# A graph, mixer and expert kernel on Trainium2: tokens go to expert-owned pages inside the graph network, sums are cleared by ScalarE, a bias add stands later

## The chip, the cores and the metric

The kernel runs on one core of a Trainium2 chip. The metric is the device time of one execution in microseconds (us), the median of several runs. The engines are TensorE (PE, with PEld for its weight loads), VectorE (DVE), ScalarE (ACT), GpSimd (POOL) and SyncE (SP), which issues most of the transfers. Every time of a stretch below is counted from the start of the profiled span.

## The reference, cut to what matters

Three parts work on 6250 tokens of 256 features: a graph network on the normalised tokens with per-node edge sums, a mixer of four layers, and at the end an expert layer that sends each token to one of 32 experts.

```
xn = layernorm(x)
x = x + gnn(xn, segment means of 106250 edge rows) + mixer(xn)     # 4 layers of linear attention and a feed-forward part
z = layernorm(x)
idx = argmax(z @ router_w.T + router_b)                            # one of 32 experts for each token
h = relu(z @ W1[idx] + b1[idx])                                    # 256 -> 64
x = x + relu(h @ W2[idx] + b2[idx])                                # 64 -> 256
```

## The kernel before, in words

Tokens lie as 50 tiles of P = 125 rows; two tiles make a group, so there are 25 groups (`GROUPS`). Each engine has its own program, and semaphores order them; nothing is scheduled by a planner. `res[P, 50, 260]` holds the residual rows with four more columns (layernorm scale and shift, token number, expert).

The mixer runs layer by layer. In its last layer each step also handles six of 153 edge segments, whose sums collect in `agg`. GpSimd clears `agg` at the start of that layer (line 795), and VectorE adds the graph network's output bias to the mixer's last bias there (`graph_bias`, line 1383), before the first group.

**The graph stage** follows. On each engine it is a loop over turns `i`, in which every step works on a group some turns behind: on GpSimd `res += x` for group `i` (line 847) and the reciprocal root for the layernorm of group `i-4` (line 850); on VectorE, the residual and statistics of group `i-4`, the shift that needs GpSimd's root (line 1787), the logits, the best expert and the one-hot `chosen` of group `i-6`; the running count `before_j` gives each token its rank within its partition's own column of experts. TensorE's products of the two graph layers fill the turn. SyncE loads `x` for group `g` when group `g-2` is used (`load_x`), and the experts' weights between (`load_experts`).

**The sort** comes after the last group: VectorE and TensorE work out the exclusive counts, the 1600-wide masks `fmask` and `fprod` and the positions `fpos_i`; then GpSimd scatters the 50 tiles in a row (line 854) into `tokens_sorted` in DRAM, in the order of the experts, without gaps. SyncE waits for all 50 (`f_scat`) before it loads anything.

**The expert loop** takes 81 segments (`FSEGS`): a tile of 125 sorted rows with one expert each. SyncE reads the first row's number and loads the tile `yin`; ScalarE normalises it to `zs` and copies the expert's weights; TensorE transposes and multiplies; VectorE adds; GpSimd scatters the rows to the output (line 864). Rows of the tile that belong to another expert get a number out of bounds (`omiss`). A tile with a border between experts is loaded once for each.

The lines that carry the order of these waits:

```
    for i in range(GROUPS + 4):                          # GpSimd, graph stage, before
        if i < GROUPS:
            pool.wait_ge(N_IN[i % 2], 16 * (i // 2 + 1))
            nc.gpsimd.tensor_tensor(pair(res, i), pair(res, i), x_in[i % 2], ALU.add).then_inc(n_x, 1)
        if i >= 4:
            pool.wait_ge(n_ve, i - 3)
            nc.gpsimd.tensor_tensor(..., gve, tail_half, ALU.pow).then_inc(n_root, 1)
    pool.wait_ge(f_posi, 1)
    for t in range(TILES): nc.gpsimd.indirect_dma_start(out=tokens_sorted, ...)
```

## Time and profile before

| | |
|---|---|
| median of 3 runs | 2889.43 us (2884.46 to 2896.06) |
| the profiled execution | 2899.41 us, its span 2897.7 us |
| TensorE busy | 2634.7 us, 91% |
| VectorE busy | 2147.9 us, 74% |
| ScalarE busy | 1578.4 us, 54% |
| GpSimd busy | 1762.0 us, 61% |
| TensorE's mean granted clock | 0.954 |

The profile is of one execution. A busy share is an average over stages that have different limits, so each stage is read by itself: a table of stretches says which engine fills one, the timeline says what an engine waited for, and the chain that ended last says which of these waits set the end.

### The profile page before, as it was taken

How to read it: one execution, taken by the hardware profiler on the slowest of the kernel's cores; microseconds unless marked ns; L12 is line 12 of the kernel's file. 1: busy time of each engine (PE TensorE's matmuls, PEld its weight loads, DVE VectorE, ACT ScalarE, POOL GpSimd, SP SyncE). 2: the span in 40 equal slices, each digit the busy share in tenths (PEclk: the TensorE clock that was granted, in tenths of full speed). 3: DMA queues.
4: the chain of work that ended last, by engine and by line, in shares of the span. 5: the costliest groups of instructions: out<-in, count | busy, mean ns of one | idle time of the engine just before them, and what ended most of it. 6: DMA issues, size and time to landing. Idle time of an engine off the chain costs nothing.

```text
span 2897.7 us, 57777 instructions
## 1 busy us (share of the span) xinstructions
PE 2634.7 (91%) x19546; PEld 2465.9 (85%) x19546; DVE 2147.9 (74%) x4892; ACT 1578.4 (54%) x3079; POOL 1762.0 (61%) x1615
## 2 busy tenths in 40 slices
PE   5888999999989999998999999799999998994398
PEld 3667899999989999998999999689999898994365
DVE  8988677777767777776777777688888886894154
ACT  0545466666636666663666666344444445762164
POOL 2045587777788777778877777555545553223565
PEclk7999999999999999999999999899999998996698
DMA  6012322222242222224223222343333332201343
GB/s 127 29 49 53 97 63 66 64 58 61 52 114 60 63 66 62 62 47 116 62 61 70 61 59 47 85 118 89 86 90 89 89 78 59 61 29 35 86 128 82
DMA packets 255569, 207.99 MB, mean 72 GB/s; under 512 B 165505, under 2 KB 194386, under 8 KB 255277
## 3 DMA queue, kind: packets, MB, share of 16 engines
q1 hardware_dynamic: 197678, 162.55, 21.6%
q0 software_dynamic: 57600, 41.75, 7.3%
q8 instruction: 160, 2.62, 0.4%
q14 instruction: 131, 1.07, 0.1%
HBM read 136.93 MB, written 70.16 MB: 71 GB/s over the span
## 4 chain that ended last, share of the span: by engine, by line
PE 62%; DVE 14%; POOL 11%; issue 9%; ACT 2%; DVEq 1%; DMA 1%; SPq 0%; another core or an unknown queue 0%; POOLq 0%; ACTq 0%
PE bank L399 57%; POOL edges_sorted L787 7%; PE bank L1915 4%; DVE hidh_lo L1391 3%; POOL tokens_sorted L854 2%; DVE xh L1355 2%; DVE scr L1265 1%; DVE oh L1588 1%; PE bank L2378 1%; POOL ehl L804 1%; DVEq L1567 1%; DVE bn L1346 1%; POOL r L765 1%; DMA queries<-qn 1%; DVE bn_x L1191 1%
## 5 line engine op out<-in xcount | busy, mean ns | idle before, releaser
L787 POOL DMA_INDIRECT edges_sorted<-staging,pos_i x850 | 1073.1, 1263 | 246.5 <-issue 230.1
L911 ACT ACTIVATE hid<-bank,b1p 128x250 f32<-128x250 f32 x800 | 331.1, 465 | 323.7 <-PE bank L399 281.1
L399 PE MATMUL bank<-w_hi,hidh_hi 128*125 128x256 f32 x1600 | 472.2, 295 | 24.1 <-DVE hidh_lo L1391 23.7
L399 PE MATMUL bank<-h_hi,w_hi 128*128 128x250 f32 x1600 | 479.7, 300 | 2.1 <-DVE h_lo L1375 1.3
L1391 DVE TENSOR_TENSOR hidh_lo<-hid,hidh_hi 128x500 fp32r<-128x500 f32 x400 | 319.5, 799 | 182.6 <-ACT hidh_hi L917 150.3
L399 PE MATMUL bank<-w_hi,hidh_lo 128*125 128x256 f32 x1600 | 454.1, 284 | 0.0
L399 PE MATMUL bank<-w_lo,hidh_hi 128*125 128x256 f32 x1600 | 452.3, 283 | 0.0
L399 PE MATMUL bank<-h_hi,w_lo 128*128 128x250 f32 x1600 | 448.9, 281 | 0.0
L399 PE MATMUL bank<-h_lo,w_hi 128*128 128x250 f32 x1600 | 445.4, 278 | 0.0
L399 PEld LDWEIGHTS bank<-w_hi,hidh_hi 128*125 128x125 f32 x1600 | 301.0, 188 | 32.9 <-DVE hidh_lo L1391 29.9
L399 PEld LDWEIGHTS bank<-h_hi,w_hi 128*128 128x128 f32 x1600 | 304.6, 190 | 6.5 <-DVE h_lo L1375 2.9
L917 ACT CAST hidh_hi<-hid 128x500 fp32r<-128x500 f32 x400 | 243.8, 610 | 117.2 <-PE bank L399 81.3
L399 PEld LDWEIGHTS bank<-h_lo,w_hi 128*128 128x128 f32 x1600 | 305.7, 191 | 1.9
L399 PEld LDWEIGHTS bank<-w_lo,hidh_hi 128*125 128x125 f32 x1600 | 300.6, 188 | 2.1
L399 PEld LDWEIGHTS bank<-h_hi,w_lo 128*128 128x128 f32 x1600 | 302.2, 189 | 0.0
L399 PEld LDWEIGHTS bank<-w_hi,hidh_lo 128*125 128x125 f32 x1600 | 299.9, 187 | 0.0
L765 POOL TENSOR_TENSOR r<-ve,minus_half 125x2 f32<-125x2 f32 x175 | 134.5, 769 | 228.8 <-DVE ve L1351 226.3
L804 POOL TENSOR_TENSOR ehl<-staging,ehl 128x512 fp32r<-128x512 f32 x103 | 139.3, 1352 | 155.4 <-ACT ehl L1003 147.6
L1588 DVE TENSOR_TENSOR oh<-iota_node,kb 128x1000 fp32r<-128x1000 f32 x153 | 192.1, 1255 | 41.0 <-POOL kb L799 40.7
L924 ACT COPY qT<-bank 128x500 f32<-128x500 f32 x100 | 57.7, 577 | 278.5 <-PE bank L1915 275.8
L399 PE MATMUL bank<-xh,ek 125*128 125x256 f32 x800 | 194.4, 389 | 6.8 <-DVE acc L1488 4.1
L399 PE MATMUL bank<-mmat,qT 128*125 128x256 f32 x800 | 190.0, 380 | 3.6 <-issue 3.6
(292 smaller groups left out, 6635.9 us busy)
## 6 DMA issues: line engine op xcount, KB each, us to landing
staging<-edges_sorted SPq DMA_DIRECT2D x103, 260.0 KB
staging<-in_edge_attr SPq DMA_DIRECT2D x50, 531.2 KB
queries<-qn SPq DMA_DIRECT2D x100, 250.0 KB
qin<-queries SPq DMA_DIRECT2D x100, 250.0 KB
edges_sorted<-staging,pos_i POOLq DMA_INDIRECT x850
rows_in<-edges_sorted SPq DMA_DIRECT2D x50, 260.0 KB
yin<-tokens_sorted SPq DMA_DIRECT2D x81, 127.0 KB
raw<-in_L_mix_W SPq DMA_DIRECT2D x8, 1024.0 KB, 5.8
```

Of the source, the lines that this page charges most:

```text
L399: return nc.tensor.matmul(o, left, right, start=start, stop=stop, skip_group_check=True)
L765: nc.gpsimd.tensor_tensor(o[:, :], ve[:, :], minus_half[:, :], ALU.pow).then_inc(done, 1)
L787: nc.gpsimd.indirect_dma_start(out=edges_sorted, out_offset=bass.IndirectOffsetOnAxis(ap=pos_i[:, i:i + 1], axis=0), in_=stage[:, slot, j, ...
L804: nc.gpsimd.tensor_tensor(ehl[n % 4][:, :, EA + 2:2 * EA + 2], rows_in[n % RIN][:, :, 0:EA], f32(ehl[n % 4][:, :, 0:EA]), ALU.subtract).th ...
L854: nc.gpsimd.indirect_dma_start(out=tokens_sorted, out_offset=bass.IndirectOffsetOnAxis(ap=fpos_i[:, t:t + 1], axis=0), in_=res[:, t, :], i ...
L911: a = nc.scalar.activation(hid[c % 2][:, j, :], chunks(PH[c % 2])[:, j, :], ACT.Gelu, bias=b1p[:, 2 * c + j:2 * c + j + 1])
L917: nc.scalar.copy(hidh[c % 2][0][:, :, :], hid[c % 2][:, :, :]).then_inc(f_hi, 1)
L924: nc.scalar.copy(qT[:, :, :], chunks(PQT)).then_inc(q_copied, 1)
L1355: a = nc.vector.tensor_scalar(o[:, j, :], res_row(PAIR * g + j), mv[:, j, 0:1], r[:, j:j + 1], ALU.subtract, ALU.mult)
L1391: nc.vector.tensor_tensor(hidh[c % 2][1][:, :, :], hid[c % 2][:, :, :], f32(hidh[c % 2][0][:, :, :]), ALU.subtract).then_inc(f_lo, 1)
L1588: nc.vector.tensor_tensor(oh[n % 4][:, :, :], iota_node[:, :].unsqueeze(1).to_broadcast((128, SEGR, P)), kb[:, n % 4, :].unsqueeze(2).to_b ...
L1915: a = nc.tensor.transpose(o[0:128, c, j * n:(j + 1) * n], i[:, j, c * 128:(c + 1) * 128], ident[0:n, 0:n])
```

## The change

It has four parts.

1. `tokens_sorted` is now 32 regions of 50 pages of 128 rows (`BIN` = 6400 rows, `YROW` = 264 columns), one region for each expert. A token's place needs only its expert and its rank within that expert, so it is known as soon as its group is routed. TensorE works out the ranks with six small BF16 products in each turn (`rank_tokens`), summed in the bank PQT; VectorE turns them into a rank and a page (`route_rank` to `route_page`), and GpSimd into an element number (`token_slots`) and scatters the tile inside the graph stage (`scatter_tile`). A scatter writes the rows of two tiles side by side, 2112 bytes for each token: its own row and, on the slot before it, a row that is overwritten later or masked. Since the slots overlap, each scatter waits until the one before it has landed. SyncE first fills page 0's slot of all regions with some row (`blank`): 128 x 32 rows.
2. After the loop only the page table is worked out, from 32 counts. The expert loop has 80 segments of 128 rows, read with a stride of 50 rows; the mask `fmiss` is worked out ahead.
3. ScalarE clears `agg`, at the end of the drain before the last layer, with a copy of zeros.
4. `graph_bias` stands behind the first group's `attention_low`.

TensorE's 48 idle products before the expert loop become 24, and no longer wait for the scatters' end.

```diff
+            blank = tokens_sorted.rearrange("(e p k) c -> p e k c", e=EXP, p=PAGE)[:, :, PAGES - 1, :]
+            sp.wait_ge(f_ones, 3)
+            sp.dma_start(blank[0:P, :, :], res[:, TILES - 1, :].unsqueeze(1).to_broadcast((P, EXP, YROW))).then_inc(blank_written, 16)
+            sp.dma_start(blank[P:PAGE, :, :], res[0:PAGE - P, TILES - 1, :].unsqueeze(1).to_broadcast((PAGE - P, EXP, YROW))).then_inc(blank_written, 16)
...
-                    nc.gpsimd.memset(agg[:, :, :], 0.0).then_inc(s_ones, 1)
...
+            def scatter_rows(at_rows, rows, done):
+                pool.wait_ge(f_scat, 16 * done)
+                nc.gpsimd.indirect_dma_start(out=token_cells, out_offset=bass.IndirectOffsetOnAxis(ap=at_rows, axis=0),
+                                             in_=rows, in_offset=None).then_inc(f_scat, 16)
+
+            def scatter_tile(t):
+                if t == 0:
+                    pool.wait_ge(blank_written, 64)
+                    scatter_rows(fpos_i[:, 0:1], res[:, 1, :], 0)
+                    scatter_rows(first_own[:, :], res[:, 0, :], 0)
+                else:
+                    scatter_rows(fpos_i[:, t:t + 1], res[:, t - 1:t + 1, :].rearrange("p t c -> p (t c)"), t + 1)
+
+            for i in range(GROUPS + 8):
+                if i >= 8:
+                    scatter_tile(PAIR * (i - 8) + 1)
...
-                if i >= 4:
+                if 4 <= i < GROUPS + 4:
                     pool.wait_ge(n_ve, i - 3)
                     nc.gpsimd.tensor_tensor(pair(res, i - 4, D + 1)[:, :, D], gve[:, :], tail_half[:, :], ALU.pow).then_inc(n_root, 1)
-            pool.wait_ge(f_posi, 1)
-            for t in range(TILES):
-                nc.gpsimd.indirect_dma_start(
...
+                if 7 <= i < GROUPS + 7:
+                    token_slots(i - 7)
+                    scatter_tile(PAIR * (i - 7))
...
+                if L == LAYERS - 1:
+                    act.wait_ge(c_ready, LAYERS)
+                    cells = agg[:, :, :].rearrange("p t c -> p (t c)")
+                    nc.scalar.copy(cells, tri[0:P, 0:1].to_broadcast((P, TILES * (2 * EA + 2)))).then_inc(s_ones, 1)
...
-                if l == LAYERS - 1 and t == -1:
-                    graph_bias()
...
                     attention_low(l, t + 1)
+                    if l == LAYERS - 1 and t == -1:
+                        graph_bias()
...
+            def route_page(g):
+                stepped()
+                if g >= 2:
+                    dve.wait_ge(f_scat, 16 * (PAIR * (g - 2) + 2))
+                nc.vector.tensor_scalar(page[:, g % 2, :], share[:, :], RND, None, ALU.add).then_inc(n_placed, 1)
...
+            def rank_tokens(g):
+                now, last = chosen[g % 2], chosen[(g + 1) % 2]
+                both = "p j e -> p (j e)"
+                pe.wait_ge(n_chosen, g + 1)
+                pe.wait_ge(n_placed, g)
```

How the instructions stand on three engines, before and after:

SyncE, at the start of the graph stage. Before:

```order
L693 DMA staging<-in_L_ffn_router_w 32x256 [waits s_add,f_res]
L694 DMA staging<-in_L_ffn_b 32x64
L695 DMA rb_b<-in_L_ffn_router_b 125x32
L632 DMA x_in<-in_x 125x512 [waits n_xn,n_x]
L699 DMA fw<-in_L_ffn_b 1x8192
L702 DMA fw<-in_L_ffn_W 128x4x64 x2
```

After:

```order
L707 DMA staging<-in_L_ffn_router_w 32x256 [waits s_add,f_res]
L708 DMA staging<-in_L_ffn_b 32x64
L709 DMA rb_b<-in_L_ffn_router_b 125x32
L723 DMA tokens_sorted<-res 125x32x264 [waits f_ones]
L724 DMA tokens_sorted<-res 3x32x264
L646 DMA x_in<-in_x 125x512 [waits n_xn,n_x]
L713 DMA fw<-in_L_ffn_b 1x8192
L716 DMA fw<-in_L_ffn_W 128x4x64 x2
```

The two writes of the blank rows now stand between the small router loads and the third group's `x_in`.

GpSimd, in the graph stage. Before, the last turns and the scatters behind them:

```order
L850 TENSOR_TENSOR res<-gve,tail_half 125x2 [waits n_ve]
L847 TENSOR_TENSOR res<-res,x_in 125x2x256 [waits n_in0]
L850 TENSOR_TENSOR res<-gve,tail_half 125x2 [waits n_ve] x5
L854 DMA tokens_sorted<-res,fpos_i 6250x260 [waits f_posi]
L854 DMA tokens_sorted<-res,fpos_i 6250x260 x46
L858 MEMSET tail_half 125x2
```

After, one turn in the middle of the stage, from an even tile's scatter to the next even tile's:

```order
L886 DMA tokens_sorted<-res,fpos_i 54067200x1 [waits f_scat,p_step]
L886 DMA tokens_sorted<-res,fpos_i 54067200x1 [waits f_scat]
L902 TENSOR_TENSOR res<-res,x_in 125x2x256 [waits n_in0]
L905 TENSOR_TENSOR res<-gve,tail_half 125x2 [waits n_ve]
L869 TENSOR_SCALAR parts<-frank 125x2 [waits n_placed]
L870 TENSOR_SCALAR parts<-res 125x2
L871 TENSOR_SCALAR parts<-page 125x2
L873 TENSOR_TENSOR parts<-parts 125x2 [waits p_step]
L875 TENSOR_TENSOR parts<-parts 125x2 [waits p_step]
L877 CAST fpos_i<-parts 125x2 [waits p_step]
L886 DMA tokens_sorted<-res,fpos_i 54067200x1 [waits f_scat,p_step]
```

The odd tile's scatter, with its wait for the one before, stands ahead of the `x` addition and of the root in the same turn; the six small operations and the even scatter stand behind.

VectorE, from the shift that needs the root to the search for the best expert's number. Before:

```order
L1787 SCALAR_TENSOR_TENSOR res<-gmv,res 125x2 [waits n_root]
L1795 TENSOR_TENSOR logit<-bank,rb_b 125x64 [waits v_step,rw_raw,n_log]
L1801 MAX best<-logit 125x8 [waits n_top]
L1801 MAX best<-logit 125x8
L1762 TENSOR_TENSOR cT_lo<-bank,cT_hi 128x500 [waits n_hi]
L1763 TENSOR_TENSOR cT_hi<-bank,cT_hi 64x250
L1757 TENSOR_TENSOR an<-asum,crec 125x256 [waits n_T,v_step]
L1806 MAX_INDEX besti<-best,logit 125x8 [waits v_step]
L1806 MAX_INDEX besti<-best,logit 125x8
```

After:

```order
L1843 SCALAR_TENSOR_TENSOR res<-gmv,res 125x2 [waits n_root]
L1875 TENSOR_TENSOR rank_j<-bank,chosen 125x64 [waits n_ranked]
L1851 TENSOR_TENSOR logit<-bank,rb_b 125x64 [waits v_step,rw_raw,n_log]
L1880 TENSOR_REDUCE frank<-rank_j 125x2 [waits v_step]
L1857 MAX best<-logit 125x8 [waits n_top]
L1857 MAX best<-logit 125x8
L1884 TENSOR_SCALAR share<-frank 125x2 [waits v_step]
L1818 TENSOR_TENSOR cT_lo<-bank,cT_hi 128x500 [waits n_hi]
L1819 TENSOR_TENSOR cT_hi<-bank,cT_hi 64x250
L1813 TENSOR_TENSOR an<-asum,crec 125x256 [waits n_T,v_step]
L1862 MAX_INDEX besti<-best,logit 125x8 [waits v_step]
L1862 MAX_INDEX besti<-best,logit 125x8
L1890 TENSOR_SCALAR page<-share 125x2 [waits f_scat,v_step]
```

Three small operations are new between the shift and `cT_lo`, and `page`, on which GpSimd's six operations wait, stands behind the search.

## Rows read from the trace of the kernel before

**Rows 1.** Busy time by stretch of the tail: us, engines, PEclk, DMA share, GB/s.
```profile
2478.00:2606.00 128.00, 128.00 (x1117) 128.00 (x1116) 116.22 (x425) 89.86 (x197) 32.34 (x31) 1.00 0.17 44
...
2650.20:2727.60 77.40, 4.88 (x26) 4.70 (x27) 1.73 (x10) 0.00 (x0) 59.15 (x51) 0.51 0.31 82
2734.80:2893.00 158.20, 145.58 (x828) 99.18 (x826) 83.50 (x324) 93.42 (x243) 96.51 (x81) 0.91 0.39 108
```

**Rows 2.** The chain that ended last, 2720 to 2745: start, us, what.
```profile
2726.45 3.90 DMA tokens_sorted<-res,fpos_i
...
2732.91 3.93 DMA yin<-tokens_sorted
```

**Rows 3.** GpSimd's timeline, graph stage: start, us, instruction [idle before <-releaser].
```profile
2461.68 0.75 POOL L850 TENSOR_TENSOR res<-gve,tail_half 125x2 f32<-125x2 f32 x1 [7.29 <-DVE gve L1783]
2462.96 1.30 POOL L847 TENSOR_TENSOR res<-res,x_in 125x512 f32<-125x512 f32 x1 [0.54 <-DMA x_in<-in_x]
...
2605.89 0.75 POOL L850 TENSOR_TENSOR res<-gve,tail_half 125x2 f32<-125x2 f32 x1 [6.19 <-DVE gve L1783]
```

**Rows 4.** VectorE's timeline in one turn of the graph stage.
```profile
2606.87 0.15 DVE L1787 SCALAR_TENSOR_TENSOR res<-gmv,res 125x2 f32<-125x2 f32 x1
...
2607.20 0.29 DVE L1801 MAX8 best<-logit 125x8 f32<-125x32 f32 x2
2608.63 0.68 DVE L1762 TENSOR_TENSOR cT_lo<-bank,cT_hi 128x500 fp32r<-128x500 f32 x1 [1.14 <-ACT cT_hi L1105]
...
2610.37 0.18 DVE L1806 FIND_INDEX8 besti<-best,logit 125x8 uint32<-125x32 f32 x1
...
2611.24 0.23 DVE L1812 TENSOR_TENSOR chosen<-iota_seg,res 125x64 f32<-125x64 f32 x1
```

**Rows 5.** GpSimd's small operations: count, ns min/median/max or mean.
```profile
L784 POOL COPY staging<-src_f x50: 203/228/761, 161.9 to 1809.1; 125x17 f32<-125x17 f32 x50
...
2723.18 0.11 POOL L858 MEMSET tail_half<- 125x2 f32 x1
```

**Rows 6.** An edge scatter, the last of its slot; the load that waits for it.
```profile
1444.03 1.18 POOL L787 DMA_INDIRECT edges_sorted<-staging,pos_i  x1 [0.31 <-issue]
...
1446.98 0.28 SPq L622 DMA_DIRECT2D staging<-in_edge_attr  x1
```

**Rows 7.** Stretches by kind of transfer, columns as in rows 1.
```profile
1852.00:1854.00 2.00, 0.00 (x0) 0.00 (x0) 0.00 (x0) 0.00 (x0) 0.00 (x0) 1.00 0.33 94
1854.00:1856.00 2.00, 0.00 (x0) 0.00 (x0) 1.27 (x3) 0.00 (x0) 0.00 (x0) 1.00 0.33 127
1847.00:1850.00 3.00, 3.00 (x20) 2.73 (x21) 1.35 (x3) 0.57 (x1) 0.00 (x0) 1.00 0.83 258
```

**Rows 8.** The third group's input: issue on SyncE, landing, use on ScalarE.
```profile
2411.68 0.26 SPq L632 DMA_DIRECT2D x_in<-in_x  x1
...
2416.82 1.27 POOL L847 TENSOR_TENSOR res<-res,x_in 125x512 f32<-125x512 f32 x1 [7.64 <-DMA x_in<-in_x]
...
2426.01 1.11 ACT L873 ACTIVATE staging<-x_in,xst 125x256 f32<-125x256 f32 x2
```

**Rows 9.** Start of the last layer: SyncE, VectorE, GpSimd, ScalarE timelines.
```profile
1857.73 3.76 SPq L544 DMA_DIRECT2D staging<-edges_sorted  x4
...
1854.65 0.43 DVE L1386 TENSOR_TENSOR b_b<-b_b,gb_b 125x256 f32<-125x256 f32 x1 [6.23 <-DMA gb_b<-in_L_gnn_b]
...
1857.85 5.50 POOL L795 MEMSET agg<- 125x6500 f32 x1
...
1868.79 0.62 ACT L1003 CAST ehl<-staging 128x512 fp32r<-128x512 f32 x1
```

**Rows 10.** TensorE's first product of a turn; VectorE's cT_lo in that turn.
```profile
2550.87 0.29 PE L399 MATMUL bank<-cT_hi,g_hi 128*128 128x250 f32 x1
...
2557.67 0.68 DVE L1762 TENSOR_TENSOR cT_lo<-bank,cT_hi 128x500 fp32r<-128x500 f32 x1
```

**Rows 11.** TensorE at the lower clock in the expert loop, columns as in rows 1.
```profile
2866.00:2881.00 15.00, 15.00 (x57) 10.10 (x56) 5.64 (x22) 7.11 (x19) 8.09 (x7) 0.54 0.21 57
```

More of the change, by code:

```diff
@@ L320, in build @@
         besti = sb("besti", [P, PAIR, 8], U32)
-        chosen = sb("chosen", [P, PAIR, EXP])
-        before_j = sb("before_j", [P, 2, PAIR, EXP])
+        chosen = [sb(f"chosen{i}", [P, PAIR, EXP], BF16) for i in range(2)]
+        tri_r = sb("tri_r", [128, 128], BF16)
+        ones_r = sb("ones_r", [128, 128], BF16)
+        rest_r = sb("rest_r", [128, 128], BF16)
+        fpos_i = sb("fpos_i", [P, TILES], I32)
+        share = sb("share", [P, PAIR])
+        page = sb("page", [P, 2, PAIR])
+        parts = sb("parts", [P, 3, PAIR])
+        first_own = sb("first_own", [P, 1], I32)
+        fcol = sb("fcol", [EXP, 6])
         rank_j = sb("rank_j", [P, PAIR, EXP])
@@ L1853, in _ @@
                     route_index(i - 6)
+                if live(7):
+                    route_page(i - 7)
                 if live(2):
@@ L1875, in _ @@
-            nc.vector.tensor_tensor(base[:, 0:EXP], base[:, 0:EXP], PS[0:P, 0:EXP], ALU.add).then_inc(sort_dve, 1)
-            nc.vector.tensor_copy(kcol[0:EXP, 0:1], PS[0:EXP, 128:129]).then_inc(sort_dve, 1)
-            dve.wait_ge(sort_dve, SORT_AT[1] + 4)
+            count, pages, start, end, big, upper = (fcol[:, i:i + 1] for i in range(6))
+            segs = iota_seg[:, 0:FSEGS]
+            step_(nc.vector.tensor_copy(count, PQT[0:EXP, 128:129]))
+            stepped()
+            step_(nc.vector.tensor_scalar(pages, count, 1.0 / PAGE, (PAGE - 1.0) / PAGE - 0.5 + 0.5 / PAGE, ALU.mult, ALU.add))
@@ new lines, in _ @@
+            dve.wait_ge(sort_pe, 5)
+            kind, begun, filled, whole = (PT[:, i * FSEGS:(i + 1) * FSEGS] for i in range(4))
+            step_(nc.vector.tensor_tensor(page_of[:, :], segs, begun, ALU.subtract))
+            step_(nc.vector.tensor_copy(fkind_i[:, :], kind[0:1, :]))
+            step_(nc.vector.tensor_scalar(first_f[:, 0, :], kind[0:1, :], float(BIN), float(PAGES - 1), ALU.mult, ALU.add))
+            stepped()
+            step_(nc.vector.tensor_tensor(first_f[:, 1, :], page_of[0:1, :], whole[0:1, :], ALU.is_lt))
@@ L2296, in route_transpose @@
                 transposes(chunks(PQ), zt, P).then_inc(n_zT, 1)
+            def rank_tokens(g):
[3 more added lines that the diff above has]
+                pe.wait_ge(n_placed, g)
+                if g:
+                    mm(PQT[0:P, 0:PAIR * EXP], rest_r[0:P, 0:P], last[:, :, :].rearrange(both), False, False)
+                    mm(PQT[0:P, 0:EXP], ones_r[0:P, 0:P], last[:, 1, :], False, False)
+                mm(PQT[0:P, 0:PAIR * EXP], tri_r[0:P, 0:P], now[:, :, :].rearrange(both), g == 0, False)
+                mm(PQT[0:P, EXP:PAIR * EXP], ones_r[0:P, 0:P], now[:, 0, :], False, False)
+                for j in range(PAIR):
+                    a = mm(PQT[0:EXP, 128:130], now[:, j, :], ones_r[0:P, 0:2], False, False)
+                a.then_inc(n_ranked, 1)
             def route_logits(g):
@@ L2315, in _ @@
             nc.tensor.transpose(PQ[0:EH, KC * EXP:(KC + 1) * EXP], fb1_r, ident[0:EXP, 0:EXP]).then_inc(gcol_pe, 1)
-            for i in range(2, GROUPS + 6):
+            for i in range(2, GROUPS + 7):
                 def live(d):
                     return 0 <= i - d < GROUPS
+                if live(7):
+                    rank_tokens(i - 7)
                 if live(2):
```

211 lines of the change are left out of this document (117 added, 94 removed).

## The prediction

> **What bounds the kernel now.** I read the table of stretches first, then the chain that ended last, then the timeline of each engine where the change acts. Between 2478 and 2606 TensorE is busy 128.00 of 128.00 us [rows 1], so the graph stage is TensorE's; GpSimd does 32.34 us there. A turn of its loop takes 8.48 us: GpSimd's root of turn 7 is at 2461.68 and that of turn 24 at 2605.89, 17 turns apart [rows 3]. VectorE has 116 of 128 us of work, so it has about 0.8 us of slack in a turn. From 2650.20 to 2727.60 GpSimd issues the 50 scatters and nothing else works. The last one starts at 2726.45 and has landed 3.90 us later, at 2730.35 [rows 2]. Then SyncE loads the first tiles, and 81 segments take 158.2 us [rows 1]. So the stretch that the change takes away is worth 77.4 us, with the sort ahead of it, if the scatters fit into the graph stage. The question is whether they do.
>
> **A turn after the change.** GpSimd's order closes a loop through VectorE. From `page` of turn i-1 to `page` of turn i these follow each other, and none can be passed by, since GpSimd and VectorE work in order:
> - handing over 0.05 us; six small operations. The nearest rows are a copy of 125x17 (203 ns least, 228 median) and a memset of 125x2 (110 ns) [rows 5]. I take 0.2 us for each, 1.2 us together; bounds 0.7 and 2.
> - a gap of 0.31 us ahead of a scatter [rows 6]; the even tile's scatter, from start to landing. It was 3.90 us for rows of 1040 bytes [rows 2]; rows are now 2112 bytes. A stretch with nothing but 125 rows of 2048 bytes moves 127 GB/s, the 125-row scatters of 1040 bytes 82 GB/s, both at a DMA share near 5 of 16 [rows 1, 7]. On five engines that is 81 against 63 ns for a row, and with 25 rows on each 0.45 us more. I take 4.4 us. Lower bound: the edge scatter with rows of 260 bytes had landed 2.95 us after its start, when SyncE issued the load that waited for it [rows 6]. Upper bound: the 2.72 us behind the issue doubled with the bytes, 6.6 us.
> - a gap of 0.31 us, and the odd tile's scatter to be issued, 1.18 us [rows 6]; its landing is off this loop.
> - the addition of `x`, 1.30 us, and the root, 0.75 us [rows 3].
> - VectorE: from the shift to the end of the two maxima 0.62 us; three inserted small operations, 0.65 us by the 0.22 us kind beside them; from `cT_lo` to the search's end 1.92 us; `page` 0.15 us. Together 3.34 us [rows 4].
>
> Sum: 0.05 + 1.2 + 0.31 + 4.4 + 0.31 + 1.18 + 1.30 + 0.75 + 3.34 = 12.84 us against 8.48. The loop holds for the 21 steps from turn 7 to turn 28 (the roots end there): 17 of 12.84 and, as the additions end with turn 24, 4 of 11.54 us, 264.5 us together.
>
> A second, shorter loop runs through TensorE: `rank_tokens` stands at the head of its turn and waits for `chosen` of the turn before. From TensorE's first product to `cT_lo` it is 6.80 us [rows 10], from there to the end of `chosen` 2.84 us [rows 4], with `page` 0.15 and six small products, estimated at 0.5 us: 10.3 us. It is hidden under the 12.84, but it is the floor of a turn even if the scatters cost nothing.
>
> **The blank rows.** They are 128 x 32 rows of 1056 bytes, 4.3 MB, and stand in SyncE's queue ahead of the third group's `x`. A transfer of 125 rows used a share of 0.33, and moved 94 GB/s (1 KB rows) or 127 GB/s (2 KB rows); one of 128 rows reached 0.83 and 258 GB/s in its stretch [rows 7]. The blank write has 125 as its outer count, so I take five engines and the 1 KB row's rate: 4.2 MB at 94 GB/s are 45 us, with the last three partitions 47. Begun at 2410.3, and with 5.14 us from issue to landing for `x` itself (2411.68 to 2416.82), the third group's `x` lands at 2462.4. ScalarE uses it at 2426.01 [rows 8]: 36 us late, and everything behind is as late, since the next loads wait for it. At 82 GB/s it would be 43 us, at 127 GB/s 24 us.
> The Trainium skill ("DMA: Bandwidth & Descriptors", the section on why a DMA increments its semaphore by 16) says that a DMA runs on the largest number of engines up to 16 that divides the outer counts of both its sides, and takes the lowest-numbered: five for 125. By that rule the share would be 0.31, and the trace has 0.31 and 0.33.
>
> **The start of the last layer.** VectorE waited 6.23 us for the bias and began the first residual at 1855; then it stood against GpSimd's 5.50 us memset of `agg` [rows 9]. Both go off the path there, some 11.7 us. But the first edge rows are issued at 1857.73 only, because they wait for the last queries, and ScalarE's first cast of edge rows, at 1868.79 [rows 9], can't be earlier than some 4 us after that issue. So 7 us are won, not 11.7; bounds 3 and 11.7. ScalarE's copy of the zeros lies in the time in which it waits there, ahead of that cast.
>
> **The sum.** Turn 7's `page` would have been at 2461.68 + 0.75 + 3.34 = 2465.8; with -7 and +36 it is at 2494.8. The first tile goes as two scatters, 1.5 us. Turn 28's `page` is at 2494.8 + 1.5 + 264.5 = 2760.8, its even scatter starts 1.5 us later. Seven scatters are left behind it, each 4.4 + 0.31 = 4.71 us after the one before, since each waits for a landing: the last starts at 2795.3 and has landed at 2799.7, against 2730.35. That is 69.3 us later. The page table (some 25 operations, mostly of the 0.22 us kind) is hidden under those seven scatters; without them it would cost some 6 us.
> In the expert loop 80 segments replace 81 (-1.6 us), the columns go from 125 to 128, and one VectorE operation of 0.2 us goes, which was not on the path. TensorE now stands idle for more than 20 us before the loop and starts it at its lower clock (1.2 GHz), where a segment took 2.9 instead of 1.6 us (five in the 15 us at 0.54) [rows 11]: some 5 us. The 128-row loads of `yin` use all engines and take away small waits, some 4 us. I set the loop at no change; bounds -28 (the 158.2 us down to 81 x 1.6) and +12.
> So the profiled execution's own time, 2899.4, becomes 2968.7. The median of the runs is 10.0 us below it, and I add the 69.3 us to the median: 2889.4 + 69.3 = 2958.7, say 2959.
>
> **The rivals.**
> - A, the above: 2959, with a range of its own of 2925 to 2995 from the bounds of the landing, the small operations and the blank. Chance 0.62.
> - B, the blank rows spread over all 16 engines, or don't hold `x` back. At the 258 GB/s of the 128-row row they take 16 us and cost some 5 instead of 36: 2928; with a landing of 2.95 us too, 42 us less (29 landings x 1.45), 2886. For it: nothing in the trace writes such a pattern. Against: all 125-row transfers show the same share. Chance 0.15, of it 0.05 within 0.5%.
> - C, faster: the root and the shift don't hold VectorE, because the scatter's landing is quick or late roots are made up. One step of a turn is worth 21 us for each us, so this decides when a turn is under 12.84 - 69.3/21 = 9.5 us. At 8.48 us a turn turn 31's `page` is 7 x 8.48 + 0.75 + 3.34 us behind the root of turn 24, at 2669.3, with -7 and +36 at 2698.3; two landings later it is 2708.9, 21 us earlier than before: 2868. Against it: the second loop alone gives 10.3 us. Chance 0.10.
> - D, the clock. TensorE works 8.5 of 12.84 us in a turn. If the pauses of 4 us put it at the lower clock for the whole stage, its products take up to 17 us a turn: 21 x 4.2 = 87 us more, 3046; for a part of each turn, some 20 us more. For it: pauses in the expert loop went with 0.54. Chance 0.07.
> - E, the expert loop gains its 28 us: 2931. Chance 0.06.
>
> The change is within 0.5% of before (what a measurement of this kernel can tell from no change) at 2875 to 2904. Faster: 0.10, from C. Same: 0.05, from B. Slower: 0.85. The range of 2895 to 3010 takes in A, B, E and the smaller form of D.
>
> **What would show it.** Right: GpSimd's roots some 12.8 us apart from turn 8 to 28, each addition of `x` behind a scatter that starts just after the landing of the one before; a wait of ScalarE for `x_in` near 2426 of some 36 us, with a DMA share of 0.3; the first `yin` load near 2801; VectorE's wait for `gb_b` gone from its place at 1848. Wrong: roots 8.5 to 10.5 us apart (C), a share near 1 for some 15 us after 2411 (B), or a granted clock well under 1 from 2520 to 2750 (D). The step I trust least is the blank rows' 36 us, then the landing.

## The result, and the profile after

The changed kernel took 2999.85 us, the median of four runs from 2996.75 to 3000.8, against 2891.35 us for the kernel before beside it. The ratio is 1.0371, with a 95% interval of 1.0354 to 1.0387. It is slower, as forecast, and 41 us over the 2959 of the forecast, inside the range. The profiled execution spans 2997.2 us, 99.5 us more than the one before.

First the table of stretches of the changed kernel: the time in which the blank rows are written, the part of it in which nothing else was issued, the turns 7 to 28, the last scatters, the experts' loop. Columns as in [rows 1].

```profile
2397.00:2443.00 46.00, 13.61 (x83) 12.68 (x82) 10.14 (x29) 7.85 (x18) 0.00 (x0) 0.61 0.36 111
...
2400.00:2432.00 32.00, 12.94 (x79) 12.09 (x79) 7.57 (x21) 5.52 (x14) 0.00 (x0) 0.66 0.34 107
...
2484.00:2798.00 314.00, 240.47 (x1574) 234.87 (x1574) 140.59 (x562) 114.63 (x247) 124.68 (x209) 0.75 0.21 56
2801.00:2844.00 43.00, 14.64 (x83) 13.48 (x83) 7.77 (x49) 0.58 (x1) 12.16 (x25) 0.58 0.16 44
2851.00:2993.00 142.00, 131.50 (x808) 90.96 (x808) 66.37 (x240) 96.95 (x240) 78.34 (x80) 0.96 0.44 123
```

In [rows 1] TensorE was busy for 128.00 of 128 us of the graph stage. Now it is busy for 240 of 314 us, and every other engine for less than half. Where no engine is full, a ring of waits can set the pace: each engine waits for the next, and the last for the first. The chain that ended last shows such a ring, here one turn of it; start, us, what.

```profile
2562.04 0.54 POOL parts L869
...
2563.85 0.20 POOL fpos_i L877
2564.05 0.66 issue
2564.71 5.54 DMA tokens_sorted<-res,fpos_i
2570.25 0.30 issue
2570.55 1.20 POOL tokens_sorted L886
2571.75 0.03 issue
2571.77 1.31 POOL res L902
2573.08 0.69 POOL res L905
2573.77 0.02 issue
2573.79 0.17 DVE res L1843
...
2576.82 0.18 DVE page L1890
2577.00 0.08 issue
2577.09 0.54 POOL parts L869
```

It is the ring of the forecast, link by link, and TensorE isn't in it. From one `parts` to the next it takes 15.05 us. The operations of line 1890 (`page`) between 2480 and 2800 are 22, those of turns 7 to 28, in the form count, ns least/median/most, first and last start. So 21 turns took 314.7 us, 15.0 us each on average (a full turn has 15.4, the last four, which have no addition, are shorter), where [rows 3] has 8.48 us.

```profile
L1890 DVE TENSOR_SCALAR page<-share x22: 168/169/171, 2483.3 to 2798.0; 125x2 f32<-125x2 f32 x22
```

The blank rows, on SyncE's queue and where ScalarE waits for the third group of `x` (both timelines, start first):

```profile
2397.07 0.31 SPq L723 DMA_DIRECT2D tokens_sorted<-res  x1
2397.42 35.14 SPq L724 DMA_DIRECT2D tokens_sorted<-res  x1
2432.66 1.69 SPq L646 DMA_DIRECT2D x_in<-in_x  x1
...
2443.28 1.09 ACT L922 ACTIVATE staging<-x_in,xst 125x256 f32<-125x256 f32 x2 [29.66 <-DMA x_in<-in_x]
```

In [rows 8] the load of `x` was issued at 2411.68. Here it is issued at 2432.66, though the stage began earlier: SyncE was held for 35.14 us at the second, small blank write (96 rows), which stands behind the first (4000 rows). The DMA share is 0.36 over this stretch, and 0.34 from 2400 to 2432, before the loads behind the blank rows add to it.

The end of the stage, the last scatters and the loads of `yin`:

```profile
L886 POOL DMA_INDIRECT tokens_sorted<-res,fpos_i x9: 1192/1197/1297, 2794.3 to 2844.3; - x9
...
L740 SPq DMA_DIRECT2D yin<-tokens_sorted x80: 5/14/681, 2850.9 to 2969.5; - x80
```

The last scatter starts at 2844.3, against 2726.45 in [rows 2], and lands 5.39 us later, at 2849.67. The first page is asked for at 2850.9. From the last landing to the end of the span are 147.5 us. Before, they were 167.4 us (2730.35 to 2897.7). So the profile's 99.5 us are 119.3 us lost up to the last landing, less 20 us in the experts' loop.

These 20 us need care. The kernel of experiment 6 has the loop of the kernel before, unchanged, and its execution spends 12 us less in it. Here is the time from the first load of `yin` to the end: before, experiment 6, changed kernel.

```profile
2731.60:2897.70 166.10, 148.78 (x856) 102.38 (x855) 83.50 (x324) 93.43 (x243) 96.56 (x81) 0.90 0.38 104
...
2716.80:2871.10 154.30, 141.55 (x856) 98.33 (x854) 84.12 (x324) 95.77 (x243) 96.62 (x81) 0.94 0.40 112
...
2850.90:2997.20 146.30, 131.50 (x808) 90.96 (x808) 66.37 (x240) 96.95 (x240) 78.34 (x80) 0.94 0.43 120
```

The profiled execution of the kernel before (2899.41 us) is slower than all its timed runs beside the changed kernel (2884.46 to 2896.06), and its loop has the stretch at a granted clock of 0.54 of [rows 11]. So the loop's gain is 8 us against one execution of the old loop and 20 us against the other.

### The profile page after: what moved, and what is told of

It is laid out like the page before. It is cut to its first block, busy times and chain, and to the rows that moved or that the text cites. A ratio compares the mean times of both kernels' runs of the same rounds, so it can differ in the third digit from the quotient of the medians.

```text
span 2997.2 us, 58012 instructions
## 1 busy us (share of the span) xinstructions
PE 2698.7 (90%) x19636; PEld 2529.2 (84%) x19636; DVE 2111.3 (70%) x4809; ACT 1586.6 (53%) x3077; POOL 1778.2 (59%) x1766
## 4 chain that ended last, share of the span: by engine, by line
PE 52%; DVE 16%; POOL 12%; issue 9%; DMA 7%; SPq 1%; ACT 1%; DVEq 1%; POOLq 0%; ACTq 0%
PE bank L413 47%; POOL edges_sorted L806 7%; DMA tokens_sorted<-res,fpos_i 6%; PE bank L1990 3%; DVE hidh_lo L1444 3%; DVE xh L1408 1%; DVE scr L1318 1%; DVE oh L1641 1%; SPq L724 1%; DVEq L1620 1%; PE bank L2466 1%; POOL ehl L822 1%; DVE bn L1399 1%; POOL tokens_sorted L886 1%; POOL r L784 1%
```

## The experiments

Each was timed beside the kernel before on the same chip, and ratios are to that kernel. Its own median lay between 2876.8 and 2887.6 us beside the experiments and at 2891.35 us beside the changed kernel. Other versions need not follow it, so the difference of two ratios from different groups of runs can be off by some 14 us, and the profiles are given where this matters. What a turn takes is read from the roots on GpSimd between 2490 and 2650 us: first to last, over their count less one. By that measure the changed kernel has 15.5 us a turn. In experiments 9 and 11 that stretch reaches into the short turns at the end of the stage, so there the full turn is given, as [rows 3] has it for the kernel before (8.48 us).

**1. The blank rows written at the program's start.** They are taken from rows of `x`, with 128 as outer count; nothing is left in the stage.

```diff
+            sp.dma_start(regions, finite).then_inc(blank_written, 16)    # behind load_up(0)
             passes(step, drain)
...
-            sp.dma_start(blank[0:P, :, :], res[:, TILES - 1, :]...).then_inc(blank_written, 16)
-            sp.dma_start(blank[P:PAGE, :, :], res[0:PAGE - P, TILES - 1, :]...).then_inc(blank_written, 16)
```

> The changed kernel, but the one blank page of each of the 32 regions (4.3 MB) is filled right after the first layer's weight loads, from rows of x in DRAM, with 128 as the outer count; nothing is left in the stage of the graph network. Theory: in the changed kernel the third group of x waited about 30 us for those rows (VectorE and GpSimd stood until 2443.3) and everything behind it moved by that, so 2970 us (2962 to 2980). Rival 1: the late turns are bound by GpSimd's chain alone and take the delay up, so the time stays within 10 us of 3000. Rival 2: the loads of the experts' weights, which follow at once, are then what the third group's successors wait for, and half comes back, 2985.

Measured: 2969.86 us, ratio 1.0274 [1.0237, 1.031]. The ratio fell by 0.0097, 28 us. The first theory stands. In the profiles it is 30 us: from the load of the router's weights to the first load of `yin` it takes 425.2 us, and 455.1 us in the changed kernel. The turn is still 15.4 us, so the later turns took nothing of the delay up.

**2. The blank rows at their place, as one transfer with 128 as the outer count.**

```diff
-            sp.dma_start(blank[0:P, :, :], res[:, TILES - 1, :].unsqueeze(1).to_broadcast((P, EXP, YROW)))...
-            sp.dma_start(blank[P:PAGE, :, :], ...)
+            regions = bass.AP(tokens_sorted.tensor, (PAGES - 1) * YROW, [[PAGES * YROW, PAGE], [BIN * YROW, EXP], [1, YROW]])
+            finite = bass.AP(x.tensor, 0, [[YROW, PAGE], [0, EXP], [1, YROW]])
+            sp.dma_start(regions, finite).then_inc(blank_written, 16)
```

> The changed kernel, the blank rows written at the same place of SyncE's queue, but with one transfer whose outer count is 128 (source rows of x in DRAM) in place of 125 and 3. Theory: with 125 as outer count the rows go through five of the sixteen engines at about 94 GB/s (some 30 us on the path); with 128 through sixteen at about 250 GB/s, 17 us, so 2984 to 2990 us. Rival: the rows of 1056 bytes are bound by memory or by the queue whatever the engines, and the time is that of the changed kernel, 3000 us. Second rival: sixteen engines busy hold x back as long as five do, since x then shares every engine: also 3000.

Measured: 2975.33 us, ratio 1.0303 [1.0265, 1.0342]. That is about 20 us under the changed kernel and 8 us over experiment 1 by the ratios, whose intervals overlap. Its stretch behind the issue:

```profile
2392.00:2404.00 12.00, 6.51 (x30) 6.00 (x31) 6.91 (x21) 4.48 (x11) 0.00 (x0) 0.50 0.89 268
...
2393.44 8.97 SPq L646 DMA_DIRECT2D x_in<-in_x  x1
```

The same 4.3 MB go at 268 GB/s with a share of 0.89, and SyncE is held for 9 us, not 35. Both rivals fall. I had set the price with all engines at 17 us, the whole time of the transfer, and 2984 to 2990 us for the kernel. The price came out at 5 to 8 us (by the medians and by the ratios; 3.4 us by the profiles, 428.6 against 425.2 us from the router's load to the first page), near the 5 us that rival B of the forecast had for it. Part of the transfer lies in the time in which nobody waits for `x`: ScalarE waits 4.26 us for it, where it waited 29.66. The Trainium skill ("DMA: Bandwidth & Descriptors", the section on why a DMA increments its semaphore by 16) gives the largest number of engines up to 16 that divides the outer counts, and so, worked out from it, five for 125 and sixteen for 128. The shares of 0.34 and 0.89 fit that. The source is different as well (DRAM, not SBUF), and one transfer stands for two, which this run doesn't separate; that the number 125 is the cause is the likely reading and not shown by itself.

**3. Single rows, and no order.** Each token writes its own row of 1056 bytes, and no scatter waits for another. Four pages of every region are made finite in layers 0 and 1, and `page` waits for the slots of two turns before and not for their scatter; an expert with more than 512 tokens would read rows never written, which doesn't occur with these inputs.

```diff
-                    scatter_rows(fpos_i[:, t:t + 1], res[:, t - 1:t + 1, :].rearrange("p t c -> p (t c)"), t + 1)
+                scatter_rows(fpos_i[:, t:t + 1], res[:, t, :], 0)
```

> Each token writes its own row only (1056 bytes, not 2112), so no two scatters touch one row and none waits for another; the rows of four pages of each region (17 MB) are made finite during layers 0 and 1 from rows of x. An expert with over 512 tokens would then read rows that nobody wrote; none has that many here. The rest is the changed kernel. Theory: the wait for the even scatter's landing (5.5 to 5.9 us in each turn) is what made the turn 15.4 us; without it the chain page, slots, two issues, add, root, VectorE is about 10.5 us, 21 turns give back some 100 us, the last eight scatters some 35 us (issue time alone), the blank rows 30 us: 2830 us (2815 to 2860). Rival 1: GpSimd's issues and VectorE's own row work share the port and the turn stays above 13 us: 2890 to 2910. Rival 2: TensorE's clock of 0.76 in this stage binds next: about 2870.

Measured: 2869.34 us, ratio 0.9928 [0.9906, 0.995], faster than the kernel before. The mechanism is right and the size was too large: a turn takes 11.9 us, not 10.5. GpSimd's wait for `page`, then TensorE's timeline (the products of two turns, the first of a turn with its wait):

```profile
2469.34 0.54 POOL L872 TENSOR_SCALAR parts<-frank 125x2 f32<-125x2 f32 x1 [3.33 <-DVE page L1887]
...
2499.43 0.41 PE L413 MATMUL bank<-cT_lo,g_hi 128*128 128x250 f32 x1
...
2507.05 0.24 PE L413 MATMUL bank<-chosen,rest_r 125*125 125x64 bf16 x1 [1.25 <-DVE chosen L1867]
...
2507.85 0.28 PE L413 MATMUL bank<-cT_hi,g_lo 128*128 128x250 f32 x1
```

The short turns are 11.3 us (the slots before these began at 2458.05): the first ring without the landing. TensorE waits for `chosen` in each turn, as it did in the changed kernel, but here this wait, the second ring of the forecast, sets some of the turns. In the turn from 2492.56 to 2506.17, 13.6 us, TensorE is at the lower level for a part (granted clock 0.53 from 2495 to 2502), the same kind of product takes 0.41 and not 0.28 us, and GpSimd waits 6.14 us for `page`. So two rings are nearly equal here, and the slower clock acts on the second.

**4. Single rows in order.** As 3, but each scatter waits for the one before.

```diff
+                scatter_rows(fpos_i[:, t:t + 1], res[:, t, :], t)
```

> As the kernel with single rows of 1056 bytes, blank pages filled in layers 0 and 1, but each scatter waits for the one before as in the changed kernel. Theory (the landing has a part that goes with bytes): with half the bytes it lands in about 4.5 us instead of 5.7, as the small edge rows did, so 21 turns by 1.2 us and 8 of the tail by 1.2 us, 35 us under the kernel with the blank rows early: 2935 us. Rival: a landing is latency whatever the bytes, so the time is that of the kernel with the blank rows early, 2970 us; the doubled row was then free and only the order cost.

Measured: 2928.85 us, ratio 1.0136 [1.0101, 1.0171], and 14.0 us a turn. Two even scatters in its chain:

```profile
2544.85 4.20 DMA tokens_sorted<-res,fpos_i
...
2558.53 4.33 DMA tokens_sorted<-res,fpos_i
```

The landings in its chain take 3.9 to 4.5 us with 1056 bytes, 4.1 in the middle (one more took 5.84), against 5.3 to 6.8 us and 5.6 in the middle with 2112 bytes. So the doubling costs some 1.5 us each time, 41 us in all (2969.9 to 2928.9), and the order alone 59.5 us more (2928.9 to 2869.3). The rival, that a landing has one price whatever the bytes, falls.

**5. The root ahead of the odd scatter.** Everything else as in the changed kernel.

```diff
             for i in range(GROUPS + 8):
-                if i >= 8:
-                    scatter_tile(PAIR * (i - 8) + 1)
                 if i < GROUPS:
...
                     nc.gpsimd.tensor_tensor(pair(res, i - 4, D + 1)[:, :, D], gve[:, :], tail_half[:, :], ALU.pow).then_inc(n_root, 1)
+                if i >= 8:
+                    scatter_tile(PAIR * (i - 8) + 1)
```

> The changed kernel with one move on GpSimd: the odd tile's scatter stands behind the add of x and the root, not ahead of them. Each scatter still waits for the one before. Theory: the root is held in each turn by the even scatter's landing; moved ahead of it, VectorE's 3.2 us and the root lie beside the landing, and the turn becomes two landings with two gaps, 2 x 5.7 + 2 x 0.3 = 12.0 us in place of 15.4: 21 turns give back 70 us, 2930 us (2915 to 2945). Rival: VectorE's and TensorE's own loop is what makes the turn, and the time stays at 3000. Second rival: the tail grows since more scatters are left at the end, and only half comes back, 2965.

Measured: 2959.51 us, ratio 1.0281 [1.026, 1.0302]. That is 26 us under the changed kernel by the ratios, but 40 us by the medians and by the first load of `yin` (2811.4 against 2850.9): the kernel before was 14.6 us faster beside this run, and the ratio carries that. 70 us were expected, so the theory's number missed. Its chain of waits between 2500 and 2690:

```profile
POOL tokens_sorted L886 <- DMA tokens_sorted<-res,fpos_i: 84.0, 27, 6.0
```

Every scatter waits for a landing now, 27 times in 190 us, while the changed kernel hid the odd landing behind add, root and VectorE. The turn is 13.4 us. The move swaps one ring (a landing and VectorE) for another (two landings), and the first `yin` load stands 61 us behind the last root, not 55. I had put the two landings at 5.7 us and both gaps at 0.3; in this chain the landings have a mean of 5.9 us, with 5.3 to 8.1, and the gap ahead of an even scatter is 0.9. That makes 13.0 us, a floor of the turn wherever the root stands, as long as the order is kept.

**6. The bias late and the clearing on ScalarE, alone.** The kernel before with these two parts.

```diff
-                if l == LAYERS - 1 and t == -1:
-                    graph_bias()
...
                     attention_low(l, t + 1)
+                    if l == LAYERS - 1 and t == -1:
+                        graph_bias()
...
-                    nc.gpsimd.memset(agg[:, :, :], 0.0).then_inc(s_ones, 1)
...
+                    nc.scalar.copy(cells, tri[0:P, 0:1].to_broadcast((P, TILES * (2 * EA + 2)))).then_inc(s_ones, 1)
```

> The kernel before with two parts of the change alone: the sums cleared by ScalarE and not by GpSimd, and the bias of the graph network made after the low half of the attention. Theory: the last layer's first GpSimd and VectorE work starts 3 to 12 us earlier, and the graph network with it; 7 us were forecast, the changed kernel's profile has its router weights asked for 13.2 us earlier: 2879 to 2882 us against 2889. Rival: the 13.2 us are the span from one execution to the next, and the time stays within 4 us of the kernel before.

Measured: 2866.43 us, ratio 0.9957 [0.9938, 0.9976], 12 us faster by the ratio (7 to 18 by the interval, 10 by the medians). SyncE's timeline, its last weight load of the layers and the router's load, then ScalarE's first cast of edge rows:

```profile
1842.12 0.40 SPq L601 DMA_DIRECT2D raw<-in_L_mix_W  x1
...
L693 SPq DMA_DIRECT2D staging<-in_L_ffn_router_w x1: 337/337/337, 2394.3 to 2394.3; - x1
...
1857.00 0.62 ACT L1002 CAST ehl<-staging 128x512 fp32r<-128x512 f32 x1 [3.88 <-DMA staging<-edges_sorted]
```

The same two rows of the kernel before:

```profile
1846.08 0.40 SPq L601 DMA_DIRECT2D raw<-in_L_mix_W  x1
...
L693 SPq DMA_DIRECT2D staging<-in_L_ffn_router_w x1: 337/337/337, 2409.0 to 2409.0; - x1
```

4 us of the earlier start lie ahead of both edits and belong to the execution. From the weight load to the router's load it is 552.2 against 562.9 us, 10.7 us less. To the first cast, which stood at 1868.79 in [rows 9], it is 14.9 against 22.7 us, 7.8 us less. Where the other 2.9 us come in isn't placed. The gain repeats: in the profiles of the changed kernel and of all its variants the stretch from this weight load to the router's load is 551.7 to 553.7 us. The rest of what this profile is shorter, 12 us, lies in the experts' loop, which the edit doesn't touch.

**7. The pages loaded as 125 and 3 rows.**

```diff
-                sp.dma_start(yin[n % YIN][:, :], token_pages[bass.ds(first, 1), :, :]...)
+                sp.dma_start(yin[n % YIN][0:P, :], rows[0:P, :]).then_inc(tokens_in(n)[0], 16)
+                sp.dma_start(yin[n % YIN][P:PAGE, :], rows[P:PAGE, :]).then_inc(tokens_in(n)[0], 16)
```

> The changed kernel, each page of the experts' part loaded with two transfers, 125 rows and 3 rows, in place of one of 128. Theory: the experts' loop fell from 161 to 142 us because a page of 128 rows comes in through sixteen engines and one of 125 through five; so the loop goes back to 155 to 162 us and the time to 3013 to 3020 us. Rival: the loop fell because one operation of VectorE is gone from each turn and what waits for it with it; the two transfers change nothing but 0.3 us of issue, 3000 us.

Measured: 3022.05 us, ratio 1.05 [1.0478, 1.0521]. The ratio is 0.0129 over the changed kernel's, 37 us, but the medians are 22 us apart and the profiled spans 24.6 us; the kernel before was faster beside this run too. The loads and the loop, then ScalarE's waits for `yin` in this kernel and in the kernel before (us in total, times, longest):

```profile
L741 SPq DMA_DIRECT2D yin<-tokens_sorted x80: 302/303/323, 2852.5 to 3000.1; - x80
...
2853.00:3017.00 164.00, 143.73 (x808) 94.67 (x808) 66.44 (x240) 93.44 (x240) 78.23 (x80) 0.96 0.35 107
...
ACT zs L924 <- DMA yin<-tokens_sorted: 50.4, 71, 1.4
...
ACT zs L873 <- DMA yin<-tokens_sorted: 5.4, 13, 0.5
```

The loop runs with the same products (x808) at 107 GB/s and not 123, and from the first load to the end it is 169 us, not 146. So two transfers for a page cost 23 us, and the rival that they change nothing falls. But they don't bring the old load back: ScalarE waits for `yin` 71 times here, 50.4 us, where with the one transfer of 125 rows it waited 13 times, 5.4 us (5 times, 3.3 us in experiment 6), and in the changed kernel not once from 2860 on. What the load of 128 rows gives by itself is therefore not shown; by these waits it is some 3 to 5 us. Another 1.6 us is the segment less. The rest of the loop's 8 to 20 us goes with TensorE's clock: the old loop has stretches of 15 to 20 us at granted clocks of 0.82, 0.84 and 0.54 in the kernel before and at 0.87 and 0.79 in experiment 6, and the changed kernel has none from 2861 to 2985 (1.00). Why not is open.

**8 to 11. Cutting the rings one after the other.** The base is experiment 3. In experiment 8, the ranks' products stand behind the first half of the up product on TensorE, and add and root stand ahead of the slots and scatters on GpSimd.

> The kernel with single rows and no order among the scatters, with two moves: on TensorE the ranks' products stand behind the first half of the up product, so that it doesn't wait for VectorE's last operation of the turn (24 us of waits in 190 us), and on GpSimd the add of x and the root stand ahead of the slots and both scatters. Theory: the turn falls from 11.9 us to that of the kernel before, 8.5 us, TensorE is busy throughout and its granted clock goes back to 2.4 GHz: 21 turns by 3.4 us, 70 us under 2869: 2800 us (2785 to 2825). Rival 1: GpSimd's issues slow VectorE's work by the port they share, and the turn is 10 us: 2830. Rival 2: the clock stays low and the turn 11 to 12 us: 2865.

Measured: 2852.71 us, ratio 0.9908 [0.9889, 0.9928], 11.5 us a turn. My theory was wrong. The slots of a turn still stood ahead of the next turn's root and waited for VectorE's `page`, so the ring was only turned, not cut. Experiment 9 cuts it:

```diff
-                if 7 <= i < GROUPS + 7:
-                    token_slots(i - 7)
-                    scatter_tile(PAIR * (i - 7))
-                    scatter_tile(PAIR * (i - 7) + 1)
+                if i >= 8:
+                    token_slots(i - 8)
+                    scatter_tile(PAIR * (i - 8))
+                    scatter_tile(PAIR * (i - 8) + 1)
```

> The kernel with single rows, no order and the add and the root ahead, with one move more on GpSimd: the slots and both scatters of a group stand one turn later, so that no add and no root is queued behind a wait for VectorE's page of the same turn. In the kernel before this one the turn stayed at 11.1 us: page, slots 2.0 with a gap of 0.7, two issues 3.1, add and root 2.0, VectorE 3.3 are still one ring, since the slots of a turn stand ahead of the next turn's root. Theory: that ring is cut, the turn falls to the 8.5 us of the kernel before, 21 turns by 2.6 us, 55 us under the former one's time less one turn at the end: ratio to the kernel before 0.972 to 0.978, 2800 to 2815 us. Rival 1: TensorE's clock and the wait for ScalarE's halves set the turn, 10.5 to 11 us: ratio 0.988. Rival 2: GpSimd's operations slow VectorE beside them by the port they share and the turn is 9.5 us: ratio 0.98.

Measured: 2836.59 us, ratio 0.9861 [0.9845, 0.9878], 10.5 us for a full turn. The ring is cut, but the time lies between the two rivals: 10.5 us is the turn of the first, but not by the clock, which is 1.00 in most turns; TensorE still waits for `chosen`. Experiment 10 is its counterpart, with the ranks' products back at the head of TensorE's turn, as in the changed kernel:

```diff
                 if live(7):
                     rank_tokens(i - 7)
                 if live(2):
                     graph_up(i - 2, 0)
```

> As the kernel with the slots one turn later, but the ranks' products at the head of TensorE's turn, where the changed kernel has them. Theory (the forecast's second ring): TensorE then waits in each turn for VectorE's last operation, and the turn is 10.3 us and not 8.5: 21 turns by 1.8 us, 38 us over the other, ratio 0.985 to 0.99. Rival: TensorE has slack for it, since the wait of 2 us stands where it would wait anyway, and the two are equal within 5 us.

Measured: 2876.49 us, ratio 0.9997 [0.9986, 1.0008], 12.6 us a turn, 39 us over the other by the ratios. The forecast's second ring is there and costs this much as soon as the first is gone. Two of its turns, root to root, with the granted clock third from the end:

```profile
2515.12:2528.72 13.60, 12.35 (x82) 12.10 (x82) 8.58 (x29) 5.95 (x13) 5.71 (x10) 0.75 0.22 52
2528.72:2539.69 10.97, 9.19 (x79) 8.93 (x79) 7.43 (x29) 5.95 (x13) 5.74 (x10) 0.96 0.32 78
```

Near the full clock the turn is 11.0 us, only 0.5 us over experiment 9; the turns with a granted clock of 0.90 take 12.7 us and those with 0.75 take 13.6 to 14.0. So most of the 39 us is the clock, acting on a ring that runs through TensorE. In experiment 11 the products stand behind the second half of the up product, with VectorE's work on ranks at the end of its turn:

```diff
                 if live(2):
                     graph_up(i - 2, 1)
+                if live(7):
+                    rank_tokens(i - 7)
                 if live(1):
                     graph_transpose(i - 1)
```

> The fastest kernel so far (single rows, no order, root ahead, slots one turn later; turn 10.2 us, ratio 0.986) with the ranks' products moved on TensorE behind the second half of the up product, and what VectorE does with the ranks moved to the end of its turn. TensorE still waited 1.3 us in each turn for the chosen experts there, and started the second half late by it. Theory: the rest of the second ring is cut and the turn falls by 1.3 us or more, to 8.5 to 8.9 us: 21 turns, 27 to 35 us, ratio 0.974 to 0.977. Rival: VectorE, slowed beside GpSimd's adds (one operation of 0.43 us takes 1.61), and ScalarE's halves set the turn, and the ratio stays at 0.985 to 0.988.

Measured: 2817.83 us, ratio 0.9752 [0.9731, 0.9773], 9.2 us for a full turn. The stretch from 2460 to 2640 in experiments 10, 9 and 11:

```profile
2460.00:2640.00 180.00, 153.65 (x1132) 149.85 (x1131) 116.52 (x403) 85.23 (x187) 85.02 (x142) 0.86 0.21 55
```

```profile
2460.00:2640.00 180.00, 161.91 (x1376) 158.01 (x1375) 144.21 (x482) 101.07 (x221) 100.79 (x170) 0.97 0.24 60
```

```profile
2460.00:2640.00 180.00, 173.13 (x1523) 170.07 (x1522) 161.45 (x547) 113.05 (x241) 112.50 (x197) 0.99 0.24 64
```

More products fit into the same time, and the granted clock climbs with them from 0.86 to 0.99. TensorE is nearly what it was in [rows 1]: the stage is its own again, with the scatters inside it. From 2460 to 2600, ahead of the stage's short last turns, it is busy 139.66 of 140 us at 1.00, so the turn is full again. Of the 0.7 us that it still has over the 8.48 us of before, the ranks' six products take some 0.5 (2507.05 to 2507.52 in experiment 3). This is the fastest version of the study, 2.5% under the kernel before. It holds for inputs in which no expert gets over 512 tokens.

## Why the forecast was right, and where its terms were off

**The direction, the two rings and what holds each link** were right. The profile shows the chain of the forecast, in its order, in 19 of the 21 turns. In one it names the odd scatter's landing (2555.54 to 2561.34), though VectorE worked without a pause from the root to `page` there too; in the last, two landings follow each other. "C, faster" is excluded (15.0 us a turn, where 9.5 decides), B by the share of 0.34 and ScalarE's wait of 29.66 us.

**The turn** was the large miss: a full turn takes 15.4 us and not 12.84, and the 21 turns 48.7 us more than forecast. Three terms make it. "I take 4.4 us" for the landing was 5.3 to 6.8 us, with a mean of 5.8 inside the turns; 3.9 to 4.5 us is the landing of the single row, as experiment 4 shows, so the step that failed is the one that charged 0.45 us for double the bytes. They cost some 1.5 us. "I take 0.2 us for each, 1.2 us together" for the six small operations was 2.0 us, since the first takes 0.54 and gaps of 0.08 lie between. And the gap of 0.31 us ahead of the even scatter was 0.66, because it follows the write of its own index; 0.30 is right for the odd one, which waited for a landing. These are 1.4 + 0.8 + 0.35 = 2.55 us a full turn. VectorE's part, forecast at 3.34, is 3.23 (2573.77 to 2577.00).

**The tail** has the same error: the scatters from 2794.3 to 2844.3 are 6.25 us apart and not 4.71, by landings of some 5.6 us, and by a gap of 0.9 us ahead of every even scatter where 0.31 was taken. From turn 28's `page` to the last landing it took 51.7 us, 13 more than forecast.

**The blank rows** were forecast at 36 us and held ScalarE 29.66 us; taken out they gave 28 us back. While nothing else was issued they moved 107 GB/s, where I had assumed 94, and by 4.2 MB that is 39 us and not 45. The share of 0.34 is near that of five engines of 16 (0.31), as assumed.

**The start of the last layer** was forecast at 7 us, with 3 to 11.7 as bounds; 10.7 us by experiment 6. I had counted the move of the first cast alone (7.8 us).

**The experts' loop** was set at no change, with a bound of -28, and gave 20 us in the profiles. I had measured it on an execution of the kernel before in which it was slow; against the old loop in experiment 6 it gave 8 us. "The 128-row loads of `yin` ... take away small waits, some 4 us" fits the 3 to 5 us of waits that went. Rival E, given 0.06, had 28 us; it came true by 8 to 20 us, and the part of that which is the clock of one execution is luck. The loop's gain is why a miss of 50 us up to the last landing (2849.7 and not 2799.7) became one of 30 us in the profile.

**Rival D**, the clock, happened without its price. The granted clock fell to 0.75 in the stage, but TensorE isn't in the ring that binds, so its slower products lie in its own waits. Two turns of the changed kernel, root to root, show it:

```profile
2526.19:2541.28 15.09, 10.16 (x55) 10.11 (x56) 8.29 (x28) 3.34 (x7) 6.07 (x11) 0.66 0.37 89
2541.28:2557.99 16.71, 13.80 (x107) 13.34 (x105) 7.44 (x29) 8.68 (x20) 6.51 (x11) 0.90 0.17 47
```

The turn at 0.66 is the shorter one; the other has a landing of 6.77 us. Where the second ring binds the clock does cost: experiment 10 has 12.6 us a turn on average and 11.0 near the full clock, where the forecast's floor at full clock was 10.3. So some 1.6 of these 2.3 us are the clock, and 0.7 us the ring itself.

**What the change gains and loses** is read best from the stretch between the load of the router's weights and the first load of `yin`, which holds the graph stage, the scatters and nothing of the loop:

| kernel | us |
|---|---|
| before | 322.6 |
| changed | 455.1 |
| blank rows early (experiment 1) | 425.2 |
| and single rows, in order (4) | 383.1 |
| and no order (3) | 325.2 |
| and add and root ahead, ranks later (8) | 312.1 |
| and slots one turn later (9) | 294.7 |
| and the ranks' products last (11) | 271.1 |

So in the changed kernel the blank rows cost 30 us, the doubled bytes 42 us and the order among the scatters 58 us. Moving the scatters under the stage by itself, in experiment 3, was even: the longer turns ate the 77 us that the scatters had alone. With both rings cut the same move is worth 51.5 us. To that come some 10 us by the bias and the clearing and 8 to 20 us in the experts' loop, which makes the 70 us that experiment 11 lies under the kernel before by the medians, and the 83 us by the profiles.

## What to carry to other kernels

To move a stretch that "nothing else uses" under a busy stage, draw the ring of each in-order engine first. The scatters had 77 us of their own and GpSimd had 96 us free, and it still lost, because a landing of 5.6 us and a handover in each turn stood ahead of something that the next turn needs. Let the moved work use the result of the turn before, so that it never waits in the ring, and after each cut look for the next ring: here the turn stopped at 15.5, 11.5 and 10.5 us before it was 9.2. And ask what a trick costs in order: writing each row twice saved a clearing, and made every scatter wait for the last. Before a gain is put down to a cause, compare with a second execution of the same code: here the loop of the kernel before took 166 us in one and 154 in another.

## What the runs showed of the hardware

- The queue that issues is held too, not only the engines that move the data: SyncE stood 35.14 us at a write of 96 rows behind one of 4000, and 8.97 us at the load behind 4096 rows with an outer count of 128.
- A scatter of 125 rows lands 3.9 to 4.5 us after its start with 1056 bytes a row (experiment 4), and 5.3 to 6.8 us with 2112 (the changed kernel).
- One operation of VectorE took 1.61 us beside an addition on GpSimd that began at the same time, where it takes 0.43 us otherwise. In experiment 9, between 2440 and 2640, three of these operations overlap an addition and took 1.54 to 1.61 us; the 15 others took 0.42 or 0.43 us. Both rows of one such pair:

```profile
2564.60 1.61 DVE L1809 TENSOR_TENSOR an<-asum,crec 125x256 f32<-125x256 f32 x1
...
2564.60 1.31 POOL L897 TENSOR_TENSOR res<-res,x_in 125x512 f32<-125x512 f32 x1
```

- An operation on 125x2 elements takes GpSimd 0.19 to 0.54 us with 0.08 us between, and a scatter that needs its result starts 0.66 us after its end.
- The same ring through TensorE took 11.0 us at a granted clock of 0.96 and 13.6 us at 0.75 (experiment 10), while the ring through GpSimd and VectorE didn't follow the clock (15.1 us at 0.66, 16.7 at 0.90).
